# Sums of rows folded by VectorE and once by TensorE, counts issued by ScalarE, and earlier reads of the residual rows in a four-layer graph kernel

## The chip, the cores and the metric

The kernel runs on one core of one Trainium2 chip. The metric is the device time of one execution in microseconds (us), the median of several. The core has TensorE (PE, with its weight loads shown as PEld), VectorE (DVE), ScalarE (ACT), GpSimd (POOL) and SyncE (SP, which only issues transfers here). ACTq and SPq in the rows are the sequencers of ScalarE and SyncE issuing DMAs.

## What is computed

`x` has 4096 rows of 64 numbers, `adj` is a sparse 4096 x 4096 matrix held dense in float32. Every layer normalises the rows, clips them at zero to h and adds a graph term to x:

```python
# layer 0: F - B*h - R*sum(h * (adj @ h))
# layer 1, two hops: x = tanh(concat([adj @ x, x]) @ W[k])
# layer 2:
mask = (adj != 0); rank = cumsum(mask, axis=1); deg = rank[:, -1:]
k = minimum(deg, 100); pos = rank - (deg - k)
w = mask * where(pos > 0, 0.5 ** (k - pos), 0)
out = w @ (h @ weight) + bias
# layer 3:
u_intra = tanh(concat([h, t]) @ W1 + b1) @ W2 + b2
u_comm = adj @ XB - sum(adj, axis=1, keepdims=True) * XB      # XB = h @ B.T
```

The change concerns three things in it: `sum(adj, axis=1)` of layer 3, the counts of non-zeros that stand for `cumsum` in layer 2, and the residual rows x that each layer adds to.

## The kernel before

The 64 MB of `adj` are read in five sweeps, one after the other: L0 (layer 0), L1A and L1B (the two hops of layer 1), L2 and L3. A sweep goes over 8 chunks (NC) of 512 result rows each. A chunk has 16 blocks (NQ) of 128 x 1024 numbers; two blocks are a pair of 1 MB, the unit of a transfer. Two or three pairs of every chunk stay in `cache` all the time, the others go through the four slots of `land`. L1A and L2 take the chunks in falling order, so that the last pairs of one sweep serve the next.

In L0, L1A, L1B and L3 a block is four matmul instructions at L1262. In L2 a block goes through three engines. VectorE makes a mask (adj != 0) in bfloat16 in one of eight buffers of `uS` (MASKS = 8) and does that six blocks ahead (LEAD = 6). TensorE multiplies it by a triangle (`triangle`, L1297), which gives every non-zero its rank within 128 columns; partition 127 of the mask's buffer holds the counts of non-zeros of the blocks that follow, so that the same matmul adds them. ScalarE, or VectorE for two blocks of a chunk, turns ranks into weights (L537, L535), and TensorE applies these three blocks later (LAG = 3, `weigh`, L1310). The counts are made in L0, kept in the DRAM tensor `counts`, and come back by a 4 KB transfer for each pair g (`counts_for`, L557), into mask buffers that the pair g - 4 has used: SP waits for `tri_done` of pair g - 4, the first four pairs wait for `sums_done`. SP issues its transfers in program order: `after_masks(g)` issues the counts of pair g + 3 between two loads of `adj` (`load`, L674), and a load waits until its slot's last users are through (`swept`, `u_ready`, `totalled`).

The sums of rows are gathered along with L1A and L1B. VectorE adds 16 of the 32 tiles of a chunk in L1A and the others in L1B to `totals(c)`, 128 x 512 float32 in the memory of `uS` (L1031, L1035; six blocks of a chunk in L1B). In L1B, after block 3 of the following chunk, TensorE multiplies `totals(c)` by a column of ones (L1160, four matmuls of two passes each, eight instructions) into `sums_p`, and VectorE writes the negated result to `rowsum` (L989), just before it adds up the hop (`hop_added`, L927, L928). The masks of L2 use the memory of the totals, and so wait for `sums_done`.

The order of all other work is written out by hand: dictionaries STAGES_* and QUICK name, for each engine alike, after which block of the following chunk a step of the epilogue of a chunk is done. Each engine runs its steps in this order. QUICK is for the first chunk of a sweep, where the sweep before has to be ended. In L1B the epilogue of a chunk is: 1 copies the sums out of PSUM (ScalarE L781) and transposes them (TensorE L1171), "added" and "tanh" end the hop, 3 adds the residual rows `xin` (VectorE L997) and starts the normalisation, which goes from VectorE (L898) to GpSimd (L690, L683, L693) and back (L916), and "turn" transposes the result (TensorE L1131). "rows" is ScalarE's read of the residual rows from DRAM into `xin` (L766): it is issued after block 1 of the following chunk, and at the start of L2 for the last chunk. `store` writes new rows (L834).

At the end of L0, "left" (VectorE L983) and "left out" (a store by ScalarE, L851) deal with the matrix column of every 128 that the triangle leaves out; for L0's last chunk they stand after block 15 of L1A's first chunk.

## Time and profile before

| | us |
|---|---|
| median of 3 runs | 733.83 |
| lowest and highest | 732.15, 735.96 |
| the profiled execution, in all | 736.61 |
| its span | 734.8 |
| TensorE, VectorE, ScalarE, GpSimd busy | 685.3, 463.5, 192.0, 113.6 |
| DMA over the span | 260.71 MB, 355 GB/s |

The profile is of one execution. A busy time counts the instructions that an engine computes with, and not those that wait or issue a transfer. Square brackets behind a row of a timeline give how long the engine stood idle before it and the work whose end let it go; where it waited for several things, the profile names the one it takes for the last.

### The profile page before, as it was taken

How to read it: one execution, taken by the hardware profiler on the slowest of the kernel's cores; microseconds unless marked ns; L12 is line 12 of the kernel's file. 1: busy time of each engine (PE TensorE's matmuls, PEld its weight loads, DVE VectorE, ACT ScalarE, POOL GpSimd, SP SyncE). 2: the span in 40 equal slices, each digit the busy share in tenths (PEclk: the TensorE clock that was granted, in tenths of full speed). 3: DMA queues.
4: the chain of work that ended last, by engine and by line, in shares of the span. 5: the costliest groups of instructions: out<-in, count | busy, mean ns of one | idle time of the engine just before them, and what ended most of it. 6: DMA issues, size and time to landing. Idle time of an engine off the chain costs nothing.

```text
span 734.8 us, 10203 instructions
## 1 busy us (share of the span) xinstructions
PE 685.3 (93%) x3680; PEld 267.3 (36%) x3680; DVE 463.5 (63%) x797; ACT 192.0 (26%) x295; POOL 113.6 (15%) x132
## 2 busy tenths in 40 slices
PE   3999999999899999999999997898988899999997
PEld 1433333333233333334344433344444433333332
DVE  7677777677888888857666767888888830000000
ACT  2101111111111111110000103687888831111111
POOL 5011001111100000002222222311222121211111
PEclk9999999999999999999999999999999999999999
DMA  8999999995699999779999994799999849999994
GB/s 358 414 414 412 414 413 413 412 412 231 222 384 409 334 377 378 327 279 369 373 393 364 346 389 180 290 402 392 358 379 367 321 176 345 412 398 406 369 390 170
DMA packets 47522, 260.71 MB, mean 355 GB/s; under 512 B 6576, under 2 KB 16560, under 8 KB 17264
## 3 DMA queue, kind: packets, MB, share of 16 engines
q1 hardware_dynamic: 38640, 252.18, 87.3%
q10 hardware_dynamic: 8832, 7.87, 3.4%
q8 instruction: 30, 0.49, 0.3%
q14 instruction: 20, 0.16, 0.1%
HBM read 254.38 MB, written 5.64 MB: 354 GB/s over the span
## 4 chain that ended last, share of the span: by engine, by line
PE 55%; DMA 31%; DVE 8%; issue 2%; POOL 2%; ACT 1%; DVEq 0%; SPq 0%; ACTq 0%
PE accA L1262 40%; DMA land<-adj_blocks 27%; DVE uS L1053 3%; PE work L1297 3%; PE accA L1310 3%; DVE uS L1035 2%; DMA xin<-x_rows 2%; PE work L1280 2%; PE work L1131 1%; PE work L1171 1%; PE work L1225 1%; POOL rstd L683 1%; PE accA L1231 1%; PE work L1206 1%; DMA wS<-weights 1%
## 5 line engine op out<-in xcount | busy, mean ns | idle before, releaser
L1262 PE MATMUL accA<-land,X 128*64 128x512 f32 x1504 | 365.6, 601 | 22.7 <-DVE X L1092 11.2
L1262 PEld LDWEIGHTS accA<-land,X 128*64 128x64 f32 x1504 | 99.6, 137 | 198.2 <-issue 140.4
L1035 DVE TENSOR_TENSOR uS<-uS,land 128x512 f32<-128x512 f32 x186 | 132.7, 714 | 28.0 <-DMA land<-adj_blocks 19.6
L1053 DVE TENSOR_SCALAR uS<-land 128x1024 bf16<-128x1024 f32 (+1 forms) x188 | 129.2, 725 | 33.4 <-DMA land<-adj_blocks 32.0
L1262 PE MATMUL accA<-cache,X 128*64 128x512 f32 x544 | 133.8, 597 | 2.9 <-ACT accS L781 2.9
L537 ACT ACTIVATE wS<-work 128x1024 uint16<-128x1024 f32 x112 | 108.0, 1029 | 23.9 <-PE work L1297 23.2
L1297 PE MATMUL work<-uS,triA 128*128 128x512 bf16 x256 | 76.0, 379 | 14.7 <-DVE uS L1053 8.8
L690 POOL TENSOR_TENSOR hS<-tS 128x256 f32<-128x256 f32 x24 | 23.6, 982 | 372.9 <-DVE tS L898 372.9
L1019 DVE TENSOR_TENSOR tS<-uS,work 128x256 f32<-128x256 f32 x8 | 3.4, 422 | 121.8 <-PE work L1171 121.8
L1310 PE MATMUL accA<-wS,X 128*128 128x512 bf16 x256 | 75.8, 379 | 0.0
L1262 PEld LDWEIGHTS accA<-cache,X 128*64 128x64 f32 x544 | 39.4, 138 | 71.2 <-issue 60.7
L781 ACT ACTIVATE accS<-accA 128x512 f32<-128x512 f32 x32 | 19.1, 596 | 159.9 <-PE accA L1262 155.5
L1053 DVE TENSOR_SCALAR uS<-cache 128x1024 bf16<-128x1024 f32 (+1 forms) x68 | 46.1, 701 | 9.2 <-DMA cache<-adj_blocks 9.0
L1280 PE MATMUL work<-uS,later 128*64 128x512 bf16 x256 | 49.1, 379 | 0.0
L1035 DVE TENSOR_TENSOR uS<-uS,cache 128x512 f32<-128x512 f32 x54 | 37.3, 691 | 2.7
L1297 PEld LDWEIGHTS work<-uS,triA 128*128 128x128 bf16 x256 | 22.0, 97 | 45.2 <-DVE uS L1053 19.9
L683 POOL TENSOR_TENSOR rstd<-var,power 128x4 f32<-128x4 f32 (+1 forms) x25 | 31.8, 1273 | 35.9 <-DVE var L904 35.9
L754 ACT ACTIVATE rowsT<-work 128x256 f32<-128x256 f32 x24 | 9.2, 385 | 103.1 <-PE work L1131 103.1
L1310 PEld LDWEIGHTS accA<-wS,X 128*128 128x128 f16 x256 | 24.9, 97 | 30.1
L1280 PEld LDWEIGHTS work<-uS,later 128*64 128x64 bf16 x256 | 16.4, 110 | 35.5 <-issue 28.2
L916 DVE TENSOR_SCALAR hS<-tS 128x256 f32<-128x256 f32 x24 | 7.1, 294 | 29.0 <-POOL tS L693 29.0
L535 DVE TENSOR_SCALAR wS<-work 128x1024 uint16<-128x1024 f32 x16 | 19.6, 1222 | 5.5 <-PE work L1297 5.3
(91 smaller groups left out, 393.1 us busy)
## 6 DMA issues: line engine op xcount, KB each, us to landing
land<-adj_blocks SPq DMA_DIRECT2D x219, 1024.0 KB, 8.1
cache<-adj_blocks SPq DMA_DIRECT2D x17, 1024.0 KB, 11.7
x_rows<-zS ACTq DMA_DIRECT2D x24, 128.0 KB, 7.3
xin<-x_rows ACTq DMA_DIRECT2D x24, 128.0 KB, 7.2
uS<-counts SPq DMA_DIRECT2D x64, 4.0 KB
out_rows<-zS ACTq DMA_DIRECT2D x8, 128.0 KB, 7.0
rows_transposed<-rowsT SPq DMA_DIRECT2D x7, 128.0 KB, 7.8
wS<-rows_transposed SPq DMA_DIRECT2D x7, 128.0 KB, 7.6
```

Source lines behind the costliest of these rows:

```text
L535: ops.tensor_scalar(w, of, 0.0, None, ALU.max).then_inc(w_ready_dve, 1)
L537: ops.activation(w, of, ACT.Relu).then_inc(w_ready, 1)
L683: nc.gpsimd.tensor_tensor(out[:, 0:ntile], of[:, 0:ntile], power[:, 0:ntile], ALU.pow)\
L690: nc.gpsimd.tensor_tensor(hS[:, :], tS[:, :], tS[:, :], ALU.mult).then_inc(rows_squared, 1)
L754: nc.scalar.activation(rowsT[:, :], tr_of(p, c), ACT.Copy).then_inc(tr_evac, 1)
L781: last = nc.scalar.activation(accS[:, :], accA[:, c % 2, :], ACT.Copy)
L1035: nc.vector.tensor_tensor(total, total, of[:, i * W:(i + 1) * W], ALU.add)\
L1053: nc.vector.tensor_scalar(masks(b)[0:rows, :], block_of(p, c, b)[0:rows, :], 0.0, None, ALU.not_equal)\
L1262: last = nc.tensor.matmul(accA[k * D:(k + 1) * D, c % 2, :], tile(X[p % 2], TQ * q + k), of[:, k * W:(k + 1) * W], start=(b == 0), stop=(b ...
L1280: last = nc.tensor.matmul(spare[k * D:(k + 1) * D, c % 2, :], later[:, NT - t:NT - t + D], masks(b)[:, k * W:(k + 1) * W], start=(b == 0), ...
L1297: last = nc.tensor.matmul(work[:, 2 * tri_pair(n) + k, :], triA[:, :], masks(b)[:, k * W:(k + 1) * W], start=True, stop=True)
L1310: last = nc.tensor.matmul(accA[:, c % 2, :], tile16(TQ * q + k), weights(n)[:, k * W:(k + 1) * W].bitcast(BF16), start=(b == 0 and k == 0) ...
```

## The change

- The column `ones` and the sums by TensorE in L1B (L1160) with their copy (L989) go. Instead VectorE, after the last block of each chunk of L1B (`fold_totals`), transposes each half of `totals(c)` in squares of 32 x 32 into `tS` and adds up each run of 32, 8 columns a half, into `part_sums`, which takes the place of the weights `hop0`, no longer needed. In the first chunk of L2, after block 12, TensorE adds the parts of all chunks up by eight small matmuls with the identity `join`, and VectorE writes the negated sums of all 32 tiles at once ("row sums").
- The waits for `sums_done` become waits for `folded`, which VectorE signals twice a chunk.
- The counts of the first four pairs are issued by SP in the last three chunks of L1B and at the start of L2. Those of all others are issued by ScalarE, behind the weights of the second block of pair g - 4, under the same condition on `tri_done`. SP's loop of counts goes.
- "rows" in L1B stands after block 12 of the chunk itself, as in L2, and not after block 1 of the next.
- "left" and "left out" of L0's last chunk stand after blocks 5 and 7 of L1A's second chunk.

`sums_p` is 32 columns wide instead of 4, and the semaphore `folded` is new. The diff, without these lines:

```diff
@@ -256,20 +255,22 @@
 HT_PE = {L0: "turn", L1A: "turn", L1B: "turn", L2: 7}
 HT_ACT = {L0: "turned", L1A: "turned", L1B: "turned", L2: 7}
-ROWS_L2 = 12
+ROWS_AT = 12
 ROW_STAGES = {"rows": 4, "hidden": 2, "tanh0": 5, "tanh1": 6, "intra": 9}
 ROW_STAGES_0 = {"rows": 11, "hidden": 9, "tanh0": 12, "tanh1": 13, "intra": 15}
 STAGES_L0 = {0: 0, 1: 2, "part": 4, "stack": 6, 3: 7, 4: 9, "counts": 10, 5: 11, "weights": 12, 6: 13, 7: 15,
              "left": 16, "turn": 17, "turned": 17, "left out": 18, "hop": 19, "hopped": 20}
 STAGES_L1A = {1: 2, "added": 4, "tanh": 6, "turn": 8, "turned": 9, "hop": 11, "hopped": 13}
 STAGES_L2 = {0: 2, "join0": 4, "join1": 5, 4: 6, 5: 8, 6: 10, 7: 13, 8: 15}
-STAGES_L1B = {"rows": 1, 1: 3, "added": 5, "tanh": 6, 3: 7, 4: 8, 5: 10, "turn": 12, "turned": 13, 6: 15, 7: 15}
+STAGES_L1B = {1: 3, "added": 5, "tanh": 6, 3: 7, 4: 8, 5: 10, "turn": 12, "turned": 13, 6: 15, 7: 15}
 QUICK = {L1A: {0: 0, 1: 1, 3: 1, 4: 1, 5: 2, 6: 4, 7: 6, "turn": 10, "turned": 10, "hop": 11, "hopped": 12, "part": 13,
-               "stack": 14, "counts": 14, "weights": 14, "left": 15, "left out": 15},
+               "stack": 14, "counts": 14, "weights": 14},
          L1B: {1: 1, "added": 2, "tanh": 3, "turn": 5, "turned": 5, "hop": 7, "hopped": 8},
-         L2: {"tanh": 0, 4: 2, 5: 4, "turn": 8, "turned": 9, 6: 10, 7: 10, 8: 11},
+         L2: {"tanh": 0, 4: 2, 5: 4, "turn": 8, "turned": 9, 6: 10, 7: 10, 8: 11,
+              "row sums": 12},
          L3: {0: 0, 1: 1, 4: 3, 5: 5, 6: 6, 7: 8, 8: 10}}
+LEFT_L1A = {"left": 5, "left out": 7}
 SUM_STAGES = {"sums": 3, "result": 7, "store": 11}
...
@@ -283,21 +284,24 @@
         found += at_block(QUICK[p], before)
         if p == L3:
             found += at_block(ROW_STAGES_0, (p, c))
-        return found + at_block({"rows": ROWS_L2}, (p, c)) if p == L2 else found
+        return found + at_block({"rows": ROWS_AT}, (p, c)) if p in (L1B, L2) else found
     if p == L3:
         return at_block(SUM_STAGES, before) + at_block(ROW_STAGES, (p, c))
     if p == L1B:
-        return at_block({8: 2}, before2) if before2 and b == 2 else at_block(STAGES_L1B, before)
+        found = at_block({8: 2}, before2) if before2 else []
+        return found + at_block(STAGES_L1B, before) + at_block({"rows": ROWS_AT}, (p, c))
     stages = {L0: STAGES_L0, L1A: STAGES_L1A, L2: STAGES_L2}[p]
     found = at_block({k: at - NQ for k, at in stages.items()}, before2) if before2 else []
     found += at_block(stages, before) if before else []
-    return found + at_block({"rows": ROWS_L2}, (p, c)) if p == L2 else found
+    if p == L1A and c == 1:
+        found += at_block(LEFT_L1A, (L0, NC - 1))
+    return found + at_block({"rows": ROWS_AT}, (p, c)) if p == L2 else found
 def early_stages(p, c, before, before2):
     if p == L2 and c == 0:
-        return [(8, before2), ("rows", before), (1, before)]
+        return [(8, before2), (1, before)]
     return []
...
@@ -536,6 +545,15 @@
             else:
                 ops.activation(w, of, ACT.Relu).then_inc(w_ready, 1)
+        def counts_of(g):
+            c, k = g // PAIRS, pair_order(L2, g // PAIRS)[g % PAIRS]
+            at = (2 * g) % MASKS * BLK
+            return (uS[LAST:P, at:at + 2 * BLK].rearrange("o (t w) -> o t w", w=W),
+                    counts_d[ch(L2, c), 4 * k:4 * k + 4, :].rearrange("(o t) w -> o t w", o=1))
         block = ctx.enter_context(nc.Block())
...
@@ -548,15 +566,8 @@
             def counts_for(g):
-                if g < MASKS // 2:
-                    sp.wait_ge(sums_done, 2 * g + 2)
-                else:
-                    sp.wait_ge(tri_done, 2 * (g - MASKS // 2) + 2)
-                c, k = g // PAIRS, pair_order(L2, g // PAIRS)[g % PAIRS]
-                at = (2 * g) % MASKS * BLK
-                sp.dma_start(uS[LAST:P, at:at + 2 * BLK].rearrange("o (t w) -> o t w", w=W),
-                             counts_d[ch(L2, c), 4 * k:4 * k + 4, :].rearrange("(o t) w -> o t w", o=1))\
-                    .then_inc(counts_in[g % (MASKS // 2)], 16)
+                sp.wait_ge(folded, 4 * g + 4)
+                sp.dma_start(*counts_of(g)).then_inc(counts_in[g % (MASKS // 2)], 16)
             def left_adjacency(c):
...
@@ -595,10 +606,6 @@
                 if issued["keep"] < NC - 2 and g >= PAIRS * (issued["keep"] + 2) + 2:
                     keep_rows(issued["keep"])
                     issued["keep"] += 1
-                for i in range(issued["counts"], min(g + AHEAD, PAIRS * NC - 1) + 1):
-                    counts_for(i)
-                    issued["counts"] = i + 1
                 if issued["left"] < NC and g >= PAIRS * (issued["left"] - 1) + 3:
                     left_over(issued["left"])
                     issued["left"] += 1
...
@@ -607,15 +614,18 @@
                     issued["left rows"] += 1
             LEFT_ROWS_AT = {NC - 3: 1, NC - 2: 3, NC - 1: 7}
-            issued = {"keep": 0, "counts": 0, "left": 2, "left rows": NC - 3}
+            issued = {"keep": 0, "left": 2, "left rows": NC - 3}
             def step(p, c, before, before2):
+                if p == L1B and c >= NC - 3:
+                    if c == NC - 3:
+                        sp.wait_ge(counts_out, 16 * NC)
+                    counts_for(c - NC + 3)
                 if p == L2 and c == 0:
-                    sp.wait_ge(counts_out, 16 * NC)
                     sp.wait_ge(left_out, 16 * NC)
                     left_over(0)
                     left_over(1)
-                    after_masks(-1)
+                    counts_for(3)
                 if p == L3 and c == 0:
                     after_masks(PAIRS * NC - 1)
                     keep_rows(NC - 2)
...
@@ -699,7 +709,7 @@
                     pool.wait_ge(nat_evac, nat_no(L3, c - 1))
                 pool.wait_ge(nat_evac, nat_no(L2, ch(L2, c), 1) + 1)
                 pool.wait_ge(rows_in, (rows_in_no(L3, c) + 1) * 16)
-                pool.wait_ge(rowsum_ready, c + 1)
+                pool.wait_ge(rowsum_ready, 1)
                 nc.gpsimd.tensor_tensor(rows4(out), rows4(chunk(X[0], c)), spread(rowsum[:, c * 4:(c + 1) * 4]),
                                         ALU.mult).then_inc(side_step, 1)
                 pool.wait_ge(side_step, 2 * c + 1)
...
@@ -853,6 +863,14 @@
             def main(p, c, b):
                 if p == L2 and b not in evac_on_dve(c):
                     weights_out(act, nc.scalar, c, b)
+                if p == L2 and b % 2:
+                    counts_for((NQ * c + b) // 2 + MASKS // 2)
+            def counts_for(g):
+                if g < PAIRS * NC:
+                    act.wait_ge(tri_done, 2 * (g - MASKS // 2) + 2)
+                    act.dma_start(*counts_of(g)).then_inc(counts_in[g % (MASKS // 2)], 16)
             def step(p, c, before, before2):
                 for k, e in early_stages(p, c, before, before2):
...
@@ -985,10 +1003,10 @@
                 elif p in (L1B, L2):
                     at = at - 1 if p == L2 and isinstance(at, int) else at
                     if at == "added":
-                        dve.wait_ge(sums_done, c + 1)
-                        nc.vector.tensor_scalar(rowsum[:, c * 4:(c + 1) * 4], sums_p, -1.0, None, ALU.mult)\
-                            .then_inc(rowsum_ready, 1)
                         hop_added()
+                    if at == "row sums":
+                        dve.wait_ge(sums_done, 1)
+                        nc.vector.tensor_scalar(rowsum[:, :], sums_p, -1.0, None, ALU.mult).then_inc(rowsum_ready, 1)
                     if at == 3:
                         rows_in_sbuf()
                         rows_written()
...
@@ -1034,6 +1052,8 @@
                             dve.wait_ge(totalled, totalled_no(p, c, b) - TQ + i)
                             nc.vector.tensor_tensor(total, total, of[:, i * W:(i + 1) * W], ALU.add)\
                                 .then_inc(totalled, 1)
+                if p == L1B and b == NQ - 1:
+                    fold_totals(c)
                 if p == L0 and (c or b >= 4):
                     mask(p, c, b)
                 if p == L2 and NQ * c + b + LEAD < NQ * NC:
...
@@ -1041,6 +1061,17 @@
                 if p == L2 and b in evac_on_dve(c):
                     weights_out(dve, nc.vector, c, b)
+            def fold_totals(c):
+                dve.wait_ge(totalled, totalled_no(L1B, c, totals_at(L1B, c)[-1]))
+                dve.wait_ge(tanh_done, tanh_no(L1A, NC - 1) + 1)
+                for h in range(2):
+                    at = (2 * c + h) * 8
+                    L(nc.vector.transpose(tS[:, :], totals(c)[:, h * CH:(h + 1) * CH]))
+                    nc.vector.tensor_reduce(part_sums[:, at:at + 8], tS[:, :].rearrange("p (n k) -> p n k", k=NT), AX_X,
+                                            ALU.add).then_inc(folded, 1)
+                    dve.wait_ge(folded, 2 * c + h + 1)
             def mask(p, c, b):
                 n = NQ * c + b
...
@@ -1048,7 +1079,7 @@
                 if n >= MASKS:
                     dve.wait_ge(counted if p == L0 else tri_done, n - MASKS + 1)
                 elif p == L2:
-                    dve.wait_ge(sums_done, b + 1)
+                    dve.wait_ge(folded, 2 * b + 2)
                 rows = P if p == L0 else LAST
                 nc.vector.tensor_scalar(masks(b)[0:rows, :], block_of(p, c, b)[0:rows, :], 0.0, None, ALU.not_equal)\
                     .then_inc(u_ready, 1)
...
@@ -1151,15 +1182,6 @@
                     if at != "join0":
                         last.then_inc(nat_done, 1)
                 if p != L2 and at == ("sums" if p == L3 else 1):
-                    if p == L1B:
-                        pe.wait_ge(totalled, totalled_no(L1B, c, totals_at(L1B, c)[-1]))
-                        tr_free(tr_no(p, c))
-                        if c:
-                            pe.wait_ge(rowsum_ready, c)
-                        for j in range(4):
-                            last = nc.tensor.matmul(sums_p[:, j:j + 1], totals(c)[:, j * P:(j + 1) * P], wt("ones"),
-                                                    start=True, stop=True)
-                        last.then_inc(sums_done, 1)
                     nat_free(nat_no(p, c, 0))
                     pe.wait_ge(acc_evac, NC * p + c + 1)
                     if p == L0:
...
@@ -1207,6 +1229,13 @@
                                                 rows_t(t % 2)[half[0]:half[1], :],
                                                 wt("hop0" if p == L0 else "hop1", rows=half), start=True, stop=True)
                     last.then_inc(hop_done, 1)
+                if at == "row sums":
+                    pe.wait_ge(folded, 2 * NC)
+                    for g in range(4):
+                        for k in range(2):
+                            last = nc.tensor.matmul(sums_p[g * NT:(g + 1) * NT, :], wt("join", k * NT, (k + 1) * NT),
+                                                    part_sums[:, g::4], start=(k == 0), stop=(k == 1))
+                    last.then_inc(sums_done, 1)
                 if at == "stack":
                     pe.wait_ge(parts_out, c + 1)
                     nc.tensor.matmul(spare[0:NT, c % 2, :], later[:, 3 * NT:4 * NT], partS[:, :],
```

## Rows read from the trace of the kernel before

**Rows 1.** The page: the span and the busy time of the engines.

```profile
span 734.8 us, 10203 instructions
...
PE 685.3 (93%) x3680; PEld 267.3 (36%) x3680; DVE 463.5 (63%) x797; ACT 192.0 (26%) x295; POOL 113.6 (15%) x132
```

**Rows 2.** Windows: length, busy by engine (PE, PEld, DVE, ACT, POOL), clock, DMA share, GB/s.

```profile
40.00:166.00 126.00, 120.93 (x774) 46.01 (x772) 90.98 (x168) 18.76 (x42) 18.14 (x18) 1.00 1.02 414
...
334.00:440.00 106.00, 102.25 (x570) 41.90 (x570) 72.07 (x131) 10.47 (x25) 23.29 (x30) 1.00 0.98 370
...
597.00:735.00 138.00, 133.44 (x646) 46.68 (x642) 9.31 (x23) 15.68 (x26) 18.76 (x27) 0.99 0.90 352
```

**Rows 3.** Timeline of TensorE in the second hop: start, duration, instruction, count.

```profile
332.84 1.05 PE L1160 MATMUL work<-wts,uS 128*128 128x1 f32 x8
...
349.38 1.05 PE L1160 MATMUL work<-wts,uS 128*128 128x1 f32 x8
350.29 0.63 PE L1171 MATMUL work<-wts,accS 128*128 128x128 f32 x4
...
435.54 1.05 PE L1160 MATMUL work<-wts,uS 128*128 128x1 f32 x8
```

**Rows 4.** Line L1318, one matmul a chunk, and windows of the masked stage.

```profile
L1318 PE MATMUL accA<-lowS,later x8: 384/385/385, 475.3 to 595.4; 32*128 32x512 bf16 x8
...
475.28:579.00 103.72, 93.69 (x445) 43.58 (x445) 87.92 (x148) 85.99 (x101) 21.37 (x23) 1.00 0.99 379
509.83:526.47 16.64, 15.71 (x76) 7.36 (x75) 14.55 (x25) 14.47 (x18) 3.64 (x4) 1.00 0.93 331
```

**Rows 5.** Timeline around one stall, all engines, and SP earlier.

```profile
480.26 1.95 SPq L557 DMA_DIRECT2D uS<-counts  x2
...
485.04 1.02 ACT L537 ACTIVATE wS<-work 128x1024 uint16<-128x1024 f32 x1
...
486.38 1.29 DVE L1053 TENSOR_SCALAR uS<-land 127x1024 bf16<-127x1024 f32 x2
...
487.30 0.59 PE L1297 MATMUL work<-uS,triA 128*128 128x512 bf16 x2 [0.78 <-DVE uS L1053]
```

**Rows 6.** VectorE by line, 334 to 450: busy, mean, idle before; and L989 once.

```profile
L1035 DVE TENSOR_TENSOR uS<-uS,cache 128x512 f32<-128x512 f32 x30 | 20.7, 690 | 1.2
...
L897 DVE TENSOR_REDUCE st<-zS 128x4 f32<-128x256 f32 x7 | 2.9, 420 | 0.2
...
L916 DVE TENSOR_SCALAR hS<-tS 128x256 f32<-128x256 f32 x7 | 2.1, 294 | 12.7 <-POOL tS L693 12.7
...
350.46 0.16 DVE L989 TENSOR_SCALAR rowsum<-work 128x4 f32<-128x4 f32 x1 [1.54 <-PE work L1160]
```

**Rows 7.** Timeline at the change to the masked stage.

```profile
455.79 0.43 DVE L997 TENSOR_TENSOR zS<-xin,natS 128x256 f32<-128x256 f32 x1 [2.55 <-DMA xin<-x_rows]
...
463.11 0.66 PE L1131 MATMUL work<-wts,hS 128*64 128x128 f32 x8 [1.47 <-DVE hS L916]
```

**Rows 8.** Issues and landings (median us; counts of L845 min/median/max), and SP's wait.

```profile
land<-adj_blocks SPq DMA_DIRECT2D x219, 1024.0 KB, 8.1
...
xin<-x_rows ACTq DMA_DIRECT2D x24, 128.0 KB, 7.2
...
DMA to landing us min/median/max: 3.8/5.0/5.6
...
SPq L557 <- PE work L1297: 78.5, 55, 2.3
```

**Rows 9.** ScalarE's timeline across a DMA issue.

```profile
518.58 1.94 ACT L537 ACTIVATE wS<-work 128x1024 uint16<-128x1024 f32 x2 [0.36 <-PE work L1297]
520.37 0.33 ACTq L766 DMA_DIRECT2D xin<-x_rows  x1
520.40 1.03 ACT L537 ACTIVATE wS<-work 128x1024 uint16<-128x1024 f32 x1
```

**Rows 10.** Timeline at the start of the first hop.

```profile
201.19 0.63 PE L1171 MATMUL work<-wts,accS 128*128 128x128 f32 x4 [1.35 <-ACT accS L781]
```

10 lines of the change are left out of this document (5 added, 5 removed).

## The prediction

> **What bounds the kernel now.** I read the page first, then the busy time by stage, then the sequences of instructions in the two stages that the change touches, and last the waits and the times to landing. The span is 734.8 us and TensorE is busy 93% of it [rows 1], so the gaps of TensorE are small and must be looked for one by one. By stage: the last stage (597 to 735) has TensorE busy 133.4 of 138 us and touches little that is changed [rows 2]; whatever ends earlier ahead of it moves it as a whole. The second hop (the code's L1B) has 102.3 of 106 us in its middle [rows 2], and the masked stage (L2) only 93.7 of 103.7 [rows 4]. The first stage runs at 414 GB/s, which I take as the DMA's ceiling; 370 GB/s in the middle of L1B is 39.2 MB in 106 us, which at the ceiling would need 94.7 us [rows 2]. The granted clock is 1.00, so it explains nothing.
>
> In L1B a chunk without a stall takes 16.54 us (from L1160 at 332.84 to the next at 349.38), and the six chunks to 435.54 take 102.70, 17.12 each: 0.58 us of each is waiting for data [rows 3]. In L2 the rows L1318, one per chunk, run from 475.3 to 595.4: 17.16 us each, over seven chunks [rows 4].
>
> **What holds up L2.** From 475.28 to 579 TensorE stands still 10.0 of 103.7 us; VectorE is busy 87.9, ScalarE 86.0, and DMA moves 379 GB/s, or 39.3 MB, 95 us at the ceiling [rows 4]. None of the three fills the time. The chunk from 509.83 to 526.47 makes this plainer: it moves only 331 GB/s and still takes 16.64 us [rows 4]. The stall at 487.30 shows why [rows 5]. TensorE was idle 0.78 us. The profile names VectorE's mask, but the masks are made six blocks ahead (LEAD) and the one at 486.38 is for a later block; ScalarE had finished its block from 485.04 by 486.06. What is left of this block's waits is the counts of its pair, which SP issued at 480.26, 7.0 us before. A pair's counts may go out only when the pair four places earlier has been used, which leaves six blocks. One matmul of this width takes 0.385 and two take 0.59 [rows 4, 5], so each further one adds 0.21 and a block of four 0.86: about 5.2 us for the six, plus small stages. A landing after 7 us is 1 to 2 us late. This I read as the main stall of L2: about 1.7 us a chunk by TensorE's idle time.
>
> **The parts, with their cost.**
> *TensorE's sums are removed in L1B.* From the first L1160 to L1171 is 0.91 us [rows 3]; a stall-free chunk falls from 16.54 to 15.63. The last chunk's share is worth nothing, since L1171 then waits for the copy of the sums by ScalarE. TensorE alone would give 6 x 0.91 = 5.5 us. What is late next: VectorE. It is busy 72.07 of 106 us, 11.6 of a 17.12 us chunk, and waits 12.7/7 = 1.8 for GpSimd in each [rows 6]. The fold adds two transposes and two reductions. A reduction of 128x256 is 0.42 [rows 6]; a transpose is in no row. Its bounds are 0.29 (L916, one source) and 0.69 (L1035, twice the elements) [rows 6], and I take 0.42, that of a reduction of the same size. With four handshakes: 1.85 us, less the 0.16 of L989 whose wait of 1.54 also goes. VectorE needs 11.6 + 1.8 + 1.7 = 15.1 us a chunk; at 0.69 each it needs 15.6. DMA needs 370/414 x 17.12 = 15.3. Three limits within half a microsecond wait for one another, so I raise today's 0.58 of waiting to 0.9: 16.5 a chunk, a gain of 0.6 x 6 = 3.6 us, between 0 and 5.5. The Trainium skill (Vector Engine (DVE) Microarchitecture Reference, section 3.8) says of the transposer that it is "Pipelined to sustain one element per cycle per lane"; by that a transpose is priced like the reduction of as many elements and the sum is the same. No row shows it.
>
> *The residual rows are asked for sooner.* At the change from L1B to L2 ScalarE issues the read late, and VectorE waits 2.55 us for it, to 455.79; GpSimd and VectorE then finish late, and TensorE waits 1.47 at 463.11 for the result [rows 7]. Issued at block 12 of the last chunk, some five blocks sooner, it is there in time. Against it: VectorE now folds the last chunk (1.85 us) before the first masks, and the hop's sums come after four masks, so the normalisation starts only about 1.4 us sooner. SP's first load in L2 waits for the same fold; those pairs are needed ten blocks later. Gain 1.8, between 0 and 4.
>
> *Counts leave SP for ScalarE's queue.* They wait for the same blocks as before, so they are not issued sooner except where SP was busy. What changes is the queue. On SP they go behind the adjacency loads, which take 8.1 us to land; on ScalarE's queue in the first stage, at a full DMA, transfers of 32 KB landed in 5.0 us (3.8 to 5.6) and the 128 KB ones take 7.2 [rows 8]. 4 KB is nearest to the 32 KB; I take 4.8, between 3.8 and 7.2. With 0.2 for the start behind an activation, 5.0 is inside the six blocks, so the 1.7 us a chunk go. SP in turn no longer waits for TensorE (78.5 us over 55 waits [rows 8]), so loads leave up to a few microseconds sooner. What is late next: VectorE at 87.9/103.7 x 17.16 = 14.5 and about 1.0 for GpSimd, 15.5; DMA at 379/414 x 17.16 = 15.7; TensorE at 93.7/103.7 x 17.16 = 15.5. I put the chunk at 16.4 with waiting among them: 0.76 x 7 = 5.3 us, between 0 and 9. ScalarE pays eight issues a chunk. The row issue at 520.37 lasts 0.33 and the activation behind it still starts at 520.40, back to back [rows 9], so a DMA issue lies under a running activation of 1.0 us; I take nothing, up to 0.33 each. GpSimd's queue is not passed by any of this.
>
> *The fold at the end.* Eight small matmuls, as pairs of passes 16 instructions with 32 columns, against eight of L1160 in 0.91 us [rows 3]: 0 to 1.8, I take 0.7, once. VectorE waits for them once in L2 with six masks in hand, which hide it.
>
> *The left-over row moves.* Today ScalarE's copy L781 is queued behind it and TensorE idles 1.35 for that copy [rows 10]. The waiting goes, but loads are late just after, so I take 0.5, between 0 and 1.35.
>
> **Sum.** 3.6 + 1.8 + 5.3 + 0.5 - 0.7 = 10.5 us off the profiled 734.8. That execution took 736.6 in all and lies 2.8 above the median of 733.8; the saving is an absolute one, so 733.8 - 10.5 = 723.3, rounded 723.5.
>
> **The rivals.**
> *The queue does not matter.* All transfers share the same DMA engines, which are busy 0.99 of L2 [rows 4]; counts on ScalarE's queue land after 7 us as well, and the stalls stay. For it: the 128 KB transfers of that queue do take 7.2 [rows 8]. Against it: the 32 KB ones took 5.0 under a fuller DMA. Of the 5.3 only 1 is left (loads sooner): 733.8 - 6.2 = 727.6. Chance 0.13. The Trainium skill (DMA: Bandwidth & Descriptors, "Issuing engines are not separate DMA queues") says that spreading transfers over engines saves only the time to issue them; that speaks for this rival. The same page's "Queues, rings and completion order" says each DMA engine takes turns between the issuing queues, which speaks against it.
>
> *The gain is given back.* VectorE and the loads take over at once: L1B keeps 1, L2 keeps 2, the change of stage 1.5, the rest nothing: 733.8 - 4.3 = 729.5. For it: the limits of 15.1 to 15.7 us are that close. Chance 0.17.
>
> *ScalarE becomes the bound of L2 (slower).* ScalarE is busy 86.0 of 103.7 us, 14.2 of a chunk. If a DMA issue is not hidden, eight of them come on top of it and of some 0.6 of waiting (my estimate). The other parts give 5.2, so the kernel is slower than now when L2's chunk passes 17.16 + 5.2/7 = 17.9 us, that is from (17.9 - 14.8)/8 = 0.39 us an issue; at 0.6 the chunk is 19.6, and the time 733.8 - 5.2 + 17 = 746. Against it: [rows 9]. Chance 0.05.
>
> *It does nothing that counts.* The sums were hidden and the stalls have another cause: 732.5. Chance 0.05.
>
> **How the numbers follow.** Forecast 0.60, then 0.13, 0.17, 0.05, 0.05. Half a per cent, 3.7 us, is about what a measurement can tell here, so faster means below 730.2. The forecast and the first rival lie there, and 0.09 of the second's 0.17: 0.82. Same: the other 0.08 and the last rival, 0.13. Slower: 0.05. The range's lower end has L2 at its 9, L1B at its 5.5 and the fold free: 723.3 - 3.7 - 1.9 - 0.7 = 717. The forecast's own upper end has L1B and the change of stage at nothing: 723.3 + 3.6 + 1.8 = 728.7. To leave out no more than 0.2 in all the range goes on to 731, which holds the first two rivals.
>
> **What would show it.** L1B: chunks of 16.3 to 16.7 us, no L1160, VectorE's transposes at about 0.42, its busy share up by a tenth, 385 GB/s. If the transposes last 1.4 or more, L1B gains nothing. L2: rows of L1318 16.4 apart instead of 17.16, and the stalls with idle activation and early masks gone; if those are still there at 0.7 to 0.9 us, three a chunk, the queue did not matter. The first normalisation in L2 ends by 461.5 less what L1B gained; ScalarE's activations stay 0.92 apart across an issue. The forecast is wrong if L2's chunk stays above 17, or if VectorE's waits for landings grow to where TensorE's idle time was.

## The result, and the profile after the change

The changed kernel takes **726.46 us** (median of nine executions, 722.26 to 730.1) against 733.83 us (nine executions on the same chip). The ratio is 0.9896, with a 95% interval of 0.9873 to 0.9919. So it is faster, by 1.0% (0.8 to 1.3), as forecast, and lies 3 us above the 723.5 that was forecast. Its profiled execution took 726.46 us, and its span is 724.7.

The page of the changed kernel, span and busy time. These lines answer to [rows 1]:

```profile
span 724.7 us, 10119 instructions
...
PE 678.8 (94%) x3619; PEld 262.1 (36%) x3632; DVE 477.8 (66%) x822; ACT 191.7 (26%) x295; POOL 116.2 (16%) x132
```

TensorE lost 6.5 us of work and VectorE gained 14.3; the span is 10.1 us shorter. Next the windows, with the columns of [rows 2]. The first line is the first stage, the second the middle of the second hop (L1B), the next three lie in the first chunk of the masked stage (L2), then comes the rest of L2, and the last stage:

```profile
40.00:166.00 126.00, 120.83 (x772) 46.16 (x772) 91.00 (x168) 18.75 (x42) 18.12 (x18) 1.00 1.02 413
330.00:433.00 103.00, 99.30 (x532) 37.01 (x530) 82.86 (x152) 10.45 (x25) 25.07 (x31) 1.00 1.00 398
448.00:452.00 4.00, 4.00 (x12) 1.54 (x12) 3.96 (x8) 2.85 (x3) 1.64 (x2) 0.57 0.89 326
461.00:465.00 4.00, 0.99 (x5) 0.32 (x4) 3.05 (x4) 1.02 (x1) 0.16 (x1) 1.00 0.65 205
465.00:469.80 4.80, 4.80 (x15) 1.67 (x13) 2.08 (x3) 3.35 (x4) 0.64 (x1) 0.64 0.87 362
469.78:573.00 103.22, 97.03 (x456) 46.29 (x466) 91.66 (x152) 89.49 (x106) 24.25 (x24) 1.00 0.98 380
590.00:724.00 134.00, 130.56 (x632) 45.86 (x628) 8.04 (x20) 15.66 (x26) 18.81 (x27) 1.00 0.92 361
```

Beside [rows 2] and [rows 4] the reader sees three things. In L1B the DMA moves 398 GB/s instead of 370 and VectorE is busy 80% of the time instead of 68%. In L2 TensorE stands still 6.2 of 103.2 us instead of 10.0. And at the change from L1B to L2 there are stretches which the kernel before does not have: four microseconds in which TensorE works one (461 to 465), and two in which its granted clock is 0.57 and 0.64.

The left-over matmul, one a chunk in L2 (it was L1318, [rows 4]), and VectorE's two new instructions in L1B, by source line (duration ns min/median/max, first and last start):

```profile
L1347 PE MATMUL accA<-lowS,later x8: 384/384/385, 469.8 to 585.7; 32*128 32x512 bf16 x8
```

```profile
L1070 DVE STREAM_TRANSPOSE tS<-uS x16: 445/445/446, 322.7 to 440.9; 128x256 f32<-128x256 f32 x16
...
L1071 DVE TENSOR_REDUCE wts<-tS x16: 419/420/420, 323.2 to 441.4; 128x8 f32<-128x256 f32 x16
```

The budget by stage is read from TensorE's rows alone: the first of the transposes of step 1 of the epilogue, once a chunk (L1171 before, L1193 after), in L1A and in L1B, and the left-over rows of L2. "Entry" is from the last of L1A to the first of L1B, "chunk" the mean of the next six in L1B, "last" the seventh distance, "change" from the last of L1B to the first left-over row, "L2 chunk" the mean of its seven, "rest" what follows, the last stage above all.

```
              to last  entry  chunk   last  L1B     change  L2     rest    span
              of L1A          (x6)          sum             chunk
before        314.20   19.55  17.12   14.58 136.8   24.25   17.16  139.4   734.8
after         313.63   17.42  16.27   13.33 128.4   27.85   16.55  139.0   724.7
difference     -0.57   -2.13  -0.85   -1.25  -8.5   +3.60   -0.61   -0.4   -10.1
forecast       -0.5            -0.6          -3.6   -1.8    -0.76   +0.7*  -10.5
```

(* the fold at the end. Its matmuls run at 459.30, within the change of stage, so the forecast for that stage is -1.8 + 0.7 = -1.1, which is 23.15 us.) The sum of the span is within half a microsecond of the forecast, but its parts are not: in these two profiles L1B gave 5 us more than forecast, the change of stage took 4.7 us more than forecast, and L2 gave 1.0 less. That needed explaining.

**Where the change of stage lost it.** ScalarE's timeline of the changed kernel (start, duration, instruction, idle before and its releaser; an ACTq line is a DMA issue):

```profile
445.65 0.42 ACT L803 ACTIVATE natS<-tS 128x256 f32<-128x256 f32 x1 [1.19 <-DVE tS L946]
...
445.97 1.92 ACT L546 ACTIVATE wS<-work 128x1024 uint16<-128x1024 f32 x2
447.76 0.24 ACTq L873 DMA_DIRECT2D uS<-counts  x1
447.78 1.03 ACT L546 ACTIVATE wS<-work 128x1024 uint16<-128x1024 f32 x1
...
455.73 0.35 ACTq L844 DMA_DIRECT2D x_rows<-zS  x1
...
459.29 1.03 ACT L546 ACTIVATE wS<-work 128x1024 uint16<-128x1024 f32 x1
462.97 0.35 ACTq L776 DMA_DIRECT2D xin<-x_rows  x1
463.43 1.02 ACT L546 ACTIVATE wS<-work 128x1024 uint16<-128x1024 f32 x1 [3.10 <-DMA x_rows<-zS]
```

TensorE over the same stretch:

```profile
444.82 0.38 PE L1326 MATMUL work<-uS,triA 128*128 128x512 bf16 x1
447.12 0.59 PE L1326 MATMUL work<-uS,triA 128*128 128x512 bf16 x2 [1.92 <-ACT wS L546]
...
448.78 1.06 PE L1339 MATMUL accA<-wS,X 128*128 128x512 bf16 x2
...
460.99 0.59 PE L1339 MATMUL accA<-wS,X 128*128 128x512 bf16 x2
464.59 0.59 PE L1326 MATMUL work<-uS,triA 128*128 128x512 bf16 x2 [3.01 <-ACT wS L546]
...
465.69 1.06 PE L1326 MATMUL work<-uS,triA 128*128 128x512 bf16 x2
```

and VectorE's before the first stall:

```profile
439.99 0.45 DVE L1070 STREAM_TRANSPOSE tS<-uS 128x256 f32<-128x256 f32 x1
...
441.41 0.42 DVE L1071 TENSOR_REDUCE wts<-tS 128x8 f32<-128x256 f32 x1
441.86 2.97 DVE L1084 TENSOR_SCALAR uS<-land 127x1024 bf16<-127x1024 f32 x4
444.75 0.41 DVE L945 TENSOR_TENSOR tS<-wS,work 128x256 f32<-128x256 f32 x1
445.19 0.42 DVE L946 TENSOR_TENSOR tS<-tS,work 128x256 f32<-128x256 f32 x1
```

There are two stalls. **Stall A**, 1.92 us at 447.12: the last hop's tanh (ACT L803) stands in ScalarE's program ahead of the weights of the second block, it needs VectorE's hop sums (L945, L946), and these stand behind the fold (1.87 us, 439.99 to 441.86) and four masks. **Stall B**, 3.01 us at 464.59: ScalarE stood still 3.10 us at the read of the residual rows (L776). That read has to come after the store of the chunk before it (L844), issued at 455.73 and landed 7.2 us later; the weights of the next block are queued behind it. Neither this store nor this read was moved by the change. They stand at the same places in the kernel before, where the store took 5.6 us to land and TensorE waited 0.76 us:

```profile
464.35 0.33 ACTq L834 DMA_DIRECT2D x_rows<-zS  x1
...
470.07 0.33 ACTq L766 DMA_DIRECT2D xin<-x_rows  x1
...
471.66 0.59 PE L1297 MATMUL work<-uS,triA 128*128 128x512 bf16 x2 [0.76 <-ACT wS L537]
```

Shortly after each stall the granted clock is 0.5 for 3.41 us, that is at the lower of its two levels, 1.2 GHz: pairs of matmuls that take 0.59 take 1.06.

### The profile page after: what moved, and what is told of

It reads as the page before. It is cut to its first block, busy times and chain, and to the rows that moved or that the text cites. A ratio compares the mean times of both kernels' runs of the same rounds, so it can differ in the third digit from the quotient of the medians.

```text
span 724.7 us, 10119 instructions
## 1 busy us (share of the span) xinstructions
PE 678.8 (94%) x3619; PEld 262.1 (36%) x3632; DVE 477.8 (66%) x822; ACT 191.7 (26%) x295; POOL 116.2 (16%) x132
## 4 chain that ended last, share of the span: by engine, by line
PE 54%; DMA 21%; DVE 17%; issue 4%; POOL 3%; ACT 1%; DVEq 0%; ACTq 0%; SPq 0%
PE accA L1291 39%; DMA land<-adj_blocks 18%; DVE uS L1053 7%; DVE uS L1084 3%; PE work L1326 3%; PE accA L1339 3%; DMA x_rows<-zS 2%; POOL rstd L693 2%; PE work L1309 2%; PE work L1193 1%; PE work L1254 1%; PE work L1162 1%; PE work L1228 1%; POOL tS L703 1%; PE accA L1260 1%
## 5 line engine op out<-in xcount | busy, mean ns | idle before, releaser
L1084 DVE TENSOR_SCALAR uS<-land 128x1024 bf16<-128x1024 f32 (+1 forms) x188 | 131.0, 736 | 31.7 <-DMA land<-adj_blocks 29.0
L1053 DVE TENSOR_TENSOR uS<-uS,land 128x512 f32<-128x512 f32 x186 | 133.3, 717 | 19.1 <-DMA land<-adj_blocks 10.2
L1326 PEld LDWEIGHTS work<-uS,triA 128*128 128x128 bf16 x256 | 23.5, 99 | 36.4 <-DVE uS L1084 10.1
L1309 PEld LDWEIGHTS work<-uS,later 128*64 128x64 bf16 x256 | 16.4, 110 | 35.4 <-issue 28.5
L857 ACT ACTIVATE rowsT<-countS,wts 32x512 uint16<-32x512 bf16 x8 | 5.8, 721 | 59.0 <-DVE countS L995 59.0
```

Of the source, the lines that this page charges most:

```text
L1053: nc.vector.tensor_tensor(total, total, of[:, i * W:(i + 1) * W], ALU.add)\
L1084: nc.vector.tensor_scalar(masks(b)[0:rows, :], block_of(p, c, b)[0:rows, :], 0.0, None, ALU.not_equal)\
L1309: last = nc.tensor.matmul(spare[k * D:(k + 1) * D, c % 2, :], later[:, NT - t:NT - t + D], masks(b)[:, k * W:(k + 1) * W], start=(b == 0), ...
L1326: last = nc.tensor.matmul(work[:, 2 * tri_pair(n) + k, :], triA[:, :], masks(b)[:, k * W:(k + 1) * W], start=True, stop=True)
```

## The experiments

Each edit is on the changed kernel, except the second, which is on the one before. "Ratio" is to the kernel before, timed on the same chip.

**1. The counts back on SP's queue (e1_counts_sp).** Is the gain of L2 that of the queue? SP issues the counts again, with its old wait:

```
             def after_masks(g):
+                for i in range(issued["counts"], min(g + 3, PAIRS * NC - 1) + 1):
+                    counts_for(i)         # sp: wait tri_done, then the DMA
+                    issued["counts"] = i + 1
...
-                if p == L2 and b % 2:     # ScalarE
-                    counts_for((NQ * c + b) // 2 + MASKS // 2)
```

> The changed kernel, with the counts of pairs 4 and up issued by SyncE again, between its loads, as before the change. Theory (counts landed late on SyncE's queue): the stalls of about 0.8 us with early masks and idle activation come back, rows of the left-over matmul in the masked stage stand about 17.1 us apart instead of 16.55, and the whole takes 4 to 5 us more than the changed kernel: 731 (0.996 of the kernel before). Rival (the queue does not matter, only the other parts do): the distance stays at 16.5 to 16.7 and the time at 726.5.

Measured: 727.88 us, ratio 0.9925 (0.9899 to 0.9952), profiled span 724.8. Its left-over rows by source, and its group of triangle matmuls (busy, mean ns, then idle before and what ended it):

```profile
L1345 PE MATMUL accA<-lowS,later x8: 384/385/385, 466.4 to 585.7; 32*128 32x512 bf16 x8
```

```profile
L1324 PE MATMUL work<-uS,triA 128*128 128x512 bf16 x256 | 76.1, 379 | 13.9 <-DVE uS L1082 6.6 <-issue 4.7 <-ACT wS L546 2.2
```

and the changed kernel's group, from its page:

```profile
L1326 PE MATMUL work<-uS,triA 128*128 128x512 bf16 x246 | 75.9, 387 | 9.2 <-ACT wS L546 5.2
```

(585.7 - 466.4)/7 = 17.05 us a chunk instead of 16.55: four fifths of the gain of L2 are gone, and with them the theory that the queue does not matter. Waits of 6.6 and 4.7 us for masks and "issue" are back; 4.9 of ScalarE's 5.2 in the changed kernel are stalls A and B.

The landings of the counts themselves show the cause: they came too late. The page of the profile gives none for them, but the traces hold the last update of the semaphore of each. From the issue to it, for the counts issued between 470 and 575 us:

```
                    issued by   number   shortest   median   longest us
before              SP          48       4.1        6.8      7.6
1 counts on SP      SP          48       3.8        6.7      8.0
after               ScalarE     51       1.8        4.5      7.8
5 SP's waits kept   ScalarE     50       3.5        4.6      8.7
8 after again       ScalarE     50       1.3        4.4      8.3
```

In experiments 2, 3, 4, 6 and 7, with ScalarE issuing, the medians are 4.5 to 4.9. So the move takes some 2 us off a typical landing, though single ones stay as late as before.

What nobody had expected: the span is that of the changed kernel all the same, because the change of stage takes 23.9 us instead of 27.85. Stall B is not there; the store landed after 4.3 us. So in this pair of profiles the counts on ScalarE's queue gave 3.5 us in L2 (7 x 0.50), and 3.9 were lost at the change of stage. That loss is not a price of the queue: experiments 3, 5 and 6 have the counts on ScalarE's queue too and take 23.1 to 23.3 there. The ratios, 0.9925 and 0.9896 for the changed kernel, have overlapping intervals.

**2. The sums left on TensorE (e2_sums_pe).** The kernel before, with the three other parts of the change:

```
-        return at_block({8: 2}, before2) if before2 and b == 2 else at_block(STAGES_L1B, before)
+        found = at_block({8: 2}, before2) if before2 else []
+        return found + at_block(STAGES_L1B, before) + at_block({"rows": ROWS_AT}, (p, c))
...
+                if p == L2 and b % 2:     # ScalarE issues the counts
+                    counts_for((NQ * c + b) // 2 + MASKS // 2)
```

> The changed kernel with only the sums of rows put back: TensorE multiplies the totals of each chunk by ones in the second hop, VectorE does not transpose and reduce. Theory (TensorE's 0.91 us a chunk were on the path there): chunks of the second hop at 17.1 us again instead of 16.3, 5 us more up to its end, and about 2 us given back at the change to the masked stage, where VectorE's fold stands ahead of the hop's sums: 729.5 in all (0.994). Rival (the sums were hidden by loads, the fold only costs): 724.5 (0.987).

Measured: 727.52 us, ratio 0.9925 (0.9899 to 0.9951), span 725.5. The middle of L1B:

```profile
330.00:433.00 103.00, 101.50 (x572) 42.71 (x572) 71.35 (x130) 10.03 (x24) 23.41 (x30) 1.00 0.99 382
```

TensorE is busy 101.5 of 103 us, the fullest of all these kernels, and L1B takes 133.3 us, 4.9 more than after the whole change. The change of stage takes 23.4, 4.5 less. So the fold is worth 4.9 us in L1B against this profile of the changed kernel, and 2.2 to 5.5 against the seven profiles that have its L1B (127.8 to 131.1, in the table below). Stall A is absent without the fold, which fits its cause; the ratios, 0.9925 and 0.9896 for the changed kernel, have overlapping intervals. (Its change of stage holds another wait, of 2.22 us, for the load ahead of the first left-over matmul.)

**3. The residual rows at their old place (e3_rows_late).**

```
-STAGES_L1B = {1: 3, ...
+STAGES_L1B = {"rows": 1, 1: 3, ...
-        return found + at_block(STAGES_L1B, before) + at_block({"rows": ROWS_AT}, (p, c))
+        return found + at_block(STAGES_L1B, before)
```

> The changed kernel with the residual rows of the second hop asked for at the old place (after block 1 of the next chunk, and at the start of the masked stage). Theory (the late read held up VectorE there by 2.5 us): the addition of residual rows at the start of the masked stage again waits 2 us or more for the read, and the time is 1 to 2 us above the changed kernel: 728 (0.992). Rival (the change of stage waits for other things, the store of the new rows and the fold, whatever the read does): 726.5 (0.990).

Measured: 728.5 us (twelve executions, 723.7 to 734.3), ratio 0.9931 (0.9902 to 0.9961), span 726.6. VectorE's wait for the rows, and the middle of L1B:

```profile
435.94 0.42 DVE L1015 TENSOR_TENSOR zS<-xin,natS 128x256 f32<-128x256 f32 x1 [1.63 <-DMA xin<-x_rows]
```

```profile
330.00:433.00 103.00, 96.49 (x518) 35.17 (x516) 80.75 (x148) 10.04 (x24) 25.20 (x30) 1.00 1.00 385
```

The expectation missed: the addition of residual rows at the start of L2 was to wait 2 us or more, and it does not wait at all, though the read is late again. It is issued at 445.45, and VectorE comes to the addition only at 450.62, behind the fold and the masks:

```profile
450.62 0.43 DVE L1015 TENSOR_TENSOR zS<-xin,natS 128x256 f32<-128x256 f32 x1
```

The wait shown above is that of the last but one chunk. The gain of this part lies in L1B, where I had put none: the six chunks take 16.71 instead of 16.27, the last one 15.26 instead of 13.33, 4.9 us in all with the entry. (The seven profiles with the changed kernel's L1B, its own and those of 1 and 4 to 8, reach from 16.15 to 16.62 and from 13.33 to 13.98, so for the chunk this is just outside what differs anyway, and for the last one well outside.) VectorE waits for the rows three times (2.9 us together; in the changed kernel never, in the kernel before 1.0 us in L1B), and TensorE waits longer for adjacency rows: 7.4 us between 326 and 450, against 3.5 to 6.4 in those seven profiles. That the one brings the other, since SP's loads go out after VectorE's use of the buffers, is argued and not shown. At the change of stage, where I had put 1.8 us for it, this kernel takes 23.2 us, no more than experiments 1, 5 and 6, which read early (23.9, 23.1, 23.3). So the early read gives nothing there. Neither stall B nor a drop of the clock is in it. The ratios, 0.9931 and 0.9896, have overlapping intervals.

**4. The store sooner (e4_store_sooner).** Against stall B: the stage that gives the store its data, six blocks earlier.

```
-"turned": 9, 6: 10, 7: 10, 8: 11,
+"turned": 9, 6: 10, 7: 4, 8: 11,
```

> The changed kernel with the store of the second hop's last new rows issued after block 4 of the masked stage's first chunk instead of after block 10. Theory: in the changed kernel ScalarE sits 3.1 us in its queue after block 12, because the read of the next residual rows has to wait for that store to land, and TensorE idles 3.0 us for ScalarE's weights; with the store sooner that idle goes, and the fall of the granted clock to half behind it too: the first left-over matmul 3 to 4 us sooner, 723 in all (0.985). Rival (loads or VectorE are late there just as well): less than 1 us, 726 (0.989).

Measured: 725.01 us, ratio 0.9893 (0.9862 to 0.9924), span 719.7. The store leaves at 447.38, and its landing takes 8.1 us, as long as ever, but nobody waits for it: stall B is gone and the change of stage takes 23.8 us instead of 27.85. That TensorE waited for this store is shown by it. The ratio, however, is that of the changed kernel (0.9896, and 0.9889 in experiment 8): the profiled execution, 721.46, is the fastest of six that reach to 728.2. So the stall is gone and no gain is shown from this edit alone.

**5. SP's waits kept, the counts on ScalarE's queue (e5_sp_waits).** In the changed kernel two things happen to L2 at once: the counts change queue, and SP no longer waits for TensorE before it issues loads. Here SP waits as before, for nothing:

```
             def after_masks(g):
+                for i in range(issued["counts"], min(g + 3, PAIRS * NC - 1) + 1):
+                    sp.wait_ge(tri_done, 2 * (i - MASKS // 2) + 2)
+                    issued["counts"] = i + 1
```

> The changed kernel, ScalarE issuing the counts, but with SyncE's old waits for the triangles put back between its loads, without a transfer. It tells the two effects of the move apart. Theory (the transfer itself was slow behind the loads in SyncE's queue): the left-over matmuls of the masked stage stay 16.5 to 16.7 us apart, and the time stays at 726 to 727 (0.990). Rival (loads that left sooner made the gain): 17.0 us or more apart, 4 us more, 730.

Measured: 725.17 us, ratio 0.9883 (0.9848 to 0.9919), span 725.8. The same two views as in experiment 1:

```profile
L1350 PE MATMUL accA<-lowS,later x8: 384/384/385, 469.1 to 586.0; 32*128 32x512 bf16 x8
```

```profile
L1329 PE MATMUL work<-uS,triA 128*128 128x512 bf16 x246 | 73.8, 379 | 10.5 <-issue 3.2 <-ACT wS L546 2.7 <-DVE uS L1087 2.6
```

16.70 us a chunk. The kernels with the changed kernel's steady L2 (the changed one, 2, 3, 4, 6, 7 and 8) take 16.43 to 16.79, so this one is not told apart from them, while 17.05 is 0.26 outside. The transfer's queue carries 0.35 by this pair of profiles; what the earlier loads give is between nothing and a quarter of a microsecond. Stall A is there (1.91 us) without a drop of the clock. Stall B is absent (the store landed after 3.5 us), and the change of stage takes 23.1 us.

**6. The hop's sums after two masks (e6_hop_first).** Against stall A:

```
-                    for b in range(4):
+                    for b in range(2):
                         mask(p, c, b)
                     epilogue("added", before)
-                    mask(p, c, 4)
+                    for b in range(2, 5):
+                        mask(p, c, b)
```

> The changed kernel with VectorE's sums of the last hop after two masks of the masked stage instead of four. Theory (the fold ahead of the masks made these sums late, ScalarE's tanh waits for them and its weights wait behind the tanh, so TensorE idles 1.9 us in front of the fourth triangle): that idle falls below 0.7 us, and the first left-over matmul is 1 to 3 us sooner, more where the granted clock no longer falls after it. In the median 1 to 2 us below the changed kernel. Rival: the third mask becomes the wait, less than 0.5 us is won.

Measured: 724.82 us, ratio 0.9871 (0.9838 to 0.9905), span 723.1. Stall A is gone; the third mask is now late by 0.78 us in its place, and the turn of the normalised rows waits 1.47. Change of stage 23.3 us, no drop of the clock, store landed after 2.6 us. So this edit alone, which leaves the store and the read where they were, has neither stall. How the two hang together is read from the order of two issues, ScalarE's store of new rows and SP's next load. In the changed kernel the load is 0.53 us ahead of the store (455.73, above):

```profile
455.20 1.54 SPq L684 DMA_DIRECT2D land<-adj_blocks  x2
```

and here the store is first:

```profile
456.20 0.35 ACTq L844 DMA_DIRECT2D x_rows<-zS  x1
...
456.36 1.54 SPq L684 DMA_DIRECT2D land<-adj_blocks  x2
```

From VectorE's addition of residual rows to this load it is 9.00 or 9.01 us in the kernel before, the changed kernel and experiments 1, 2, 3, 5, 6 and 8. From the same addition to the store it is 8.56 to 8.85 us in those that keep the full clock there, and 9.53 and 9.51 in the two profiles of the changed kernel, where the clock drops behind stall A. So where the clock drops, TensorE and with it ScalarE's store come 0.7 us or more later, the load goes first, and the store lands after 7.2 and 7.8 us instead of 2.6 to 4.3 (5.6 in the kernel before). Every profile with the store at its old place fits this chain. It is read from the order of events, and not shown by a run that changes the order of the two issues alone.

**7. Both, and the tanh one block later (e7_all_three).** Edits 4 and 6, and

```
-         L2: {"tanh": 0, 4: 2,
+         L2: {"tanh": 1, 4: 2,
```

> The changed kernel with the store after block 4, the hop's sums after two masks, and the tanh behind the weights of the second block. Theory: both new idle times of TensorE at the change of stage go (1.9 and 3.0 us), and the fall of the clock with them; the change of stage takes 22 to 23 us from the transposes to the first left-over matmul, against 27.9 in the changed kernel and 24.3 before: 721 in all (0.983). Rival (something else is late there, loads above all): 25 us or more, 725 (0.988).

Measured: **723.36 us** (six executions, 722.14 to 723.73), ratio 0.9857 (0.9828 to 0.9886), span 721.4. The places of the two stalls in TensorE's timeline:

```profile
446.06 0.59 PE L1327 MATMUL work<-uS,triA 128*128 128x512 bf16 x2 [0.32 <-ACT wS L546]
447.28 0.59 PE L1327 MATMUL work<-uS,triA 128*128 128x512 bf16 x2 [0.19 <-ACT wS L546]
...
453.67 0.66 PE L1163 MATMUL work<-wts,hS 128*64 128x128 f32 x8 [1.47 <-DVE hS L934]
...
462.91 0.59 PE L1327 MATMUL work<-uS,triA 128*128 128x512 bf16 x2 [0.31 <-DVE wS L544]
```

The weights of the second block are late by 0.32 and 0.19 us instead of 1.92, and the 3.01 us of stall B are gone. No idle time of TensorE over 1.5 us is left at the change of stage, which takes 22.7 us. The forecast for this stage was 24.25 - 1.8 + 0.7 = 23.15, but for another reason, as is told below.

**8. The changed kernel again (e8_changed_again),** on the chip of experiments 5 to 7, so that there is a neighbour to compare them with; no edit.

> The changed kernel once more, on the chip of the other three. Theory (the two idle times at the change of stage belong to the kernel): a span within 2 us of 725, 26 to 28 us from the transposes to the first left-over matmul, TensorE's idle of 1.9 us there again, and of 3 us again if the store takes 7 us to land. Rival (they were a chance of that one execution): 24 us or less, and no idle above 1 us. The ratio to the kernel before stays at 0.987 to 0.992.

Measured: 726.0 us (six executions, 723.68 to 728.19), ratio 0.9889 (0.9854 to 0.9925), span 726.0. TensorE's timeline at the two stalls:

```profile
447.25 1.01 PE L1326 MATMUL work<-uS,triA 128*128 128x512 bf16 x2 [1.93 <-ACT wS L546]
...
465.35 1.01 PE L1326 MATMUL work<-uS,triA 128*128 128x512 bf16 x2 [3.66 <-ACT wS L546]
```

Both stalls are there again, at the same places (B with 3.66 us, its store landed after 7.8), the clock drops at both again, and the change of stage takes 29.4 us. The chunk of L2 is 16.43. So the loss is not a chance of one execution, though it need not be in every one. The mean granted clock of whole executions bears this out for the drops: it is 0.998 to 1.0 in all seventeen of experiments 2, 6 and 7, which have no stall A, and 0.997 or less in five of the nine of the changed kernel and in five of the six here. Against this neighbour experiment 7 is 2.6 us faster: five of its six executions are below the fastest of the changed kernel's six, and the sixth is 0.05 above it. The intervals of the two ratios overlap, so the size of the gain, of which the stages show 5 to 6.7 us in the profiled executions, is known only roughly.

The stages of all of them, with the columns of the table above:

```
                      entry  chunk  last   L1B    change  L2 chunk  rest   span
after                 17.42  16.27  13.33  128.4  27.85   16.55     139.0  724.7
1 counts on SP        17.42  16.36  13.34  128.9  23.94   17.05     139.1  724.8
2 sums on TensorE     18.53  16.74  14.35  133.3  23.38   16.57     140.4  725.5
3 rows late           17.76  16.71  15.26  133.3  23.24   16.79     139.2  726.6
4 store sooner        17.42  16.15  13.53  127.8  23.78   16.65     139.2  719.7
5 SP's waits kept     17.42  16.62  13.91  131.0  23.08   16.70     139.9  725.8
6 hop's sums sooner   18.39  16.41  13.54  130.4  23.26   16.65     139.9  723.1
7 both, tanh later    18.19  16.48  13.98  131.1  22.71   16.67     139.1  721.4
8 after again         17.42  16.36  13.62  129.2  29.43   16.43     139.3  726.0
```

The changed kernel, 1 and 4 to 8 run the same program in L1B, since the edits of 1 and 5 come later, and still differ there by 0.47 us a chunk (16.15 to 16.62). This is how far one profiled execution can be trusted for a stage; smaller differences are no evidence here. The end of L1A, up to which all nine run the same program, lies at 311.8 to 315.0 us in them (314.2 in the kernel before).

## Why the prediction was right, and where it was not

**L1B: right in its mechanism; the size of the waiting is not settled.** Removing 0.91 us of TensorE from each chunk gave 0.85 in the first profile (17.12 to 16.27), and 0.50 to 0.97 over the seven profiles that have this program (16.15 to 16.62), where 0.6 was forecast. The prices were right: the transpose took 0.445 where I took 0.42, the reduction 0.420. The step "Three limits within half a microsecond wait for one another, so I raise today's 0.58 of waiting to 0.9" gave 16.5 us. The waiting measured is 16.27 - 15.63 = 0.64 in the first profile and 0.52 to 0.99 in the seven, so 0.9 was on the high side, but one profile can't refute it. VectorE at 80% and DMA at 398 GB/s, 96% of the first stage's 413, added little to it. I had counted the early read of the residual rows at the change of stage only, though it is issued in every chunk. In experiment 3 the chunk is 16.71 without it. The Trainium skill (Vector Engine (DVE) Microarchitecture Reference, section 3.8), weighed in the prediction, holds here: 256 elements a lane in 445 ns against 420 for the reduction of as many.

The entry and the last chunk gave another 3.4 us which the sum did not have. In the entry 0.91 are the sums and 1.00 a wait for an adjacency landing which is not there in the changed kernel (in experiments 6 and 7, with the same program, it is there again with 0.74 and 0.55); in the last chunk a landing wait of 0.83 is gone as well. As forecast, the last transposes now wait for ScalarE's copy: 1.05 us, it was 0.29. Over the seven profiles the whole of L1B gave 5.7 to 9.0 us, against 3.6 forecast.

**The change of stage: wrong, and with the wrong sign.** I forecast -1.8, or -1.1 with the fold's end; it was +3.6. Two steps failed.

The first is the gain of 1.8 for the early read. VectorE's wait of 2.55 us is gone as forecast, but it is gone in experiment 3 as well, where the read is late: the fold keeps VectorE busy until the rows are there. From the last transposes to the addition of the rows it is 4.2 us in the changed kernel and 4.0 in experiment 3, against 4.8 before. So the read gives nothing there that a run shows.

The second is a term that was not in the sum. The prediction had both facts: "VectorE now folds the last chunk (1.85 us) before the first masks", and "the hop's sums come after four masks". It followed them to the normalisation only, and not to ScalarE's queue, where the tanh that needs these sums stands ahead of weights that TensorE needs. That is stall A. Stall B is not the moved read. It is a store and a read that the change did not touch, with 0.76 us of the same wait already in the kernel before. It grew to 3.0 us, as the order of issues tells it, because the store fell behind SP's load when the clock had dropped (experiment 6). Experiment 6 removes stall A, and both stalls and the drops are gone; experiment 4 moves the store, and stall B is gone; with both and the tanh moved (7) the stage takes 22.7 us. That this is near the forecast is chance: the edits of 7 are not in the changed kernel, and the forecast's reason was the read.

Of the 5.1 us between the changed kernel and experiment 7, 3.0 are stall B by itself. Stall A is in experiments 1, 3, 4 and 5 too (1.91 to 1.93 us), whose change of stage is 23.1 to 23.9, 0.4 to 1.2 above experiment 7, so by itself it costs about a microsecond at most. In experiment 4 the clock drops once behind stall A, and the stage is no longer than in experiment 1 without a drop, 23.8 and 23.9. What is left of the 3.9 us between experiment 1 and the changed kernel, 0.9, would then be the drop behind stall B. That split is worked out, and not shown by a run of its own.

**L2: right.** 16.4 was forecast and 16.55 and 16.43 measured (16.43 to 16.79 in all seven profiles), and the rows that were named have changed as they should: the stalls with idle activation and early masks are gone. The landing that the forecast rests on, "I take 4.8, between 3.8 and 7.2", has medians of 4.4 to 4.9 us, with single ones up to 8.7. The first rival, that the queue does not matter, has fallen by experiment 1 (17.05) and by these landings. Experiment 5 says how the gain divides: most of it is the queue; SP's earlier loads, which the first rival priced at 1 us in all, give about that or nothing. The Trainium skill (DMA: Bandwidth & Descriptors, "Issuing engines are not separate DMA queues") holds that spreading transfers over engines saves issue time only. For bandwidth no run here contradicts it, since L2's 379 and 380 GB/s are the same. For the delay of a 4 KB transfer behind 1 MB loads it does not hold: with SP's waits unchanged that is worth 0.35 us a chunk, 17.05 to 16.70. The same page's "Queues, rings and completion order", by which each DMA engine takes turns between queues, agrees with that. But the other queue is no shield for every transfer: the store of stall B is on ScalarE's queue and lands late when SP's load was issued just ahead of it.

What is next in L2, the turn waiting for VectorE's normalised rows, was not named as such. The third rival, ScalarE as the bound, is out: its activations run on across the issues of counts (two from 445.97 for 1.92 us, an issue at 447.76 beneath them, and the next activation at 447.78). The rival that the gain is given back came true at the change of stage only, and by waits that it did not name. (Its own sum is 0.2 off: 1 + 2 + 1.5 are 4.5 and not 4.3.)

**The small terms.** The left-over row's move takes away TensorE's wait of 1.35 us for the copy, as forecast. Whether the time fell by it is not shown: the end of L1A came 0.57 us sooner (forecast 0.5), but nine profiles with this move scatter there by 3.2 us. The fold's end is 16 small matmuls in 0.46 us (forecast 0.7).

**From the profiled execution to the median.** The span fell by 10.1 us, the median by 7.4. The profiled execution of the kernel before lay 2.8 us above its median, and that of the changed one lies on its own. The step "the saving is an absolute one, so 733.8 - 10.5" took the whole distance over to the median. The excess of that one execution was, in part, stalls of the kind that the change removes, and an execution at the median has fewer of them to lose. That is an inference from two executions. What is shown is the scatter: nine of the changed kernel run from 722.3 to 730.1.

The errors cancelled: L1B gave 4.9 us more than forecast, the change of stage 4.7 less, L2 1.0 less, and the last part of the kernel 0.4 for which nothing was forecast. A forecast of the span that is good to 0.4 us was luck in its parts.

## What to carry to other kernels

When work is added to one engine, follow the delay through the program order of every engine that waits for it, at the first and the last chunk of each stage separately: here VectorE's fold delayed a tanh, and the weights behind the tanh in ScalarE's program delayed TensorE. The steady state was forecast to 0.15 us a chunk in L2 and 0.23 in L1B, and the one transition was wrong by 5. A read of rows that were just stored needs its store issued 8 us or more ahead, by the longest landing of this store seen here (8.1). Ask also which of two queues issues first there: 0.7 us decided it. Before a wait is priced as a gain, ask whether the rest of the change hides it anyway; putting back one part alone (experiment 3) shows it. Small transfers on which an engine soon waits did better on a queue without long loads in front (medians of 4.5 us instead of 6.8), with the total bandwidth the same.
